# Block rounds of a recurrence and a choice of experts: the inverse of the denominators by an integer guess, a logarithm and an exponential, with the quotient ahead of the choice

## The chip, the cores and the metric

The kernel runs on one core of one Trainium2 chip. The metric is the device time of one execution in microseconds (us). Three runs of the kernel before took 3029.61, 3036.44 and 3038.48 us, median 3036.44.

## The reference

Six layers act in turn on x, 64 x 64 tokens (4096) of 256 channels: a gated linear attention, a recurrence over each sequence, a mixture of 8 experts, a windowed attention, an attention over heads, and a gated perceptron. What the change touches is the second, a weighted mean over the past with per-channel decay w and bonus u:

```python
def step(carry, kv_t):
    p, q, o = carry
    kt, vt = kv_t
    no = jnp.maximum(o, u + kt)
    A = jnp.exp(o - no)
    E = jnp.exp(u + kt - no)
    y = (A * p + E * vt) / (A * q + E)
    no2 = jnp.maximum(w + o, kt)
    A2 = jnp.exp(w + o - no2)
    E2 = jnp.exp(kt - no2)
    return ((A2 * p + E2 * vt, A2 * q + E2, no2), y)
...
x = x + _L0_xattn_ref(64, 64, 256, L0_xattn_w, L0_xattn_u, _layernorm(x, axis=-1), ctx_2048)
x = x + _L0_ffn_ref(_layernorm(x, axis=-1), ...)   # router: logits, top 2 of 8 experts, softmax of the two
```

The choice of experts for a token needs the finished y of that token: it goes into x, x is normalised, and the router is a product with the result.

## The kernel before

The program has four parts one after another. The first layer takes about half of the span. Then come the block rounds (function `recurrence_and_experts`), in which the recurrence and the router are computed together, then the experts' tiles, then layer one. The edit lies in the block rounds, and in one point it reaches into the experts' stage.

**Blocks and rounds.** The 4096 tokens are 8 blocks of 512 tokens (8 sequences of 64). In SBUF a block of the recurrence is a tile of 128 partitions by 1024 elements: 2 groups of 128 channels, 8 sequences, 64 steps. There are ten rounds, written out by the list `STEPS`. In the round i, three blocks are at work: f = i (the front: normalise, transpose, exponentials of the keys), y = i - 1 (the scans, the inverse, the quotient) and r = i - 2 (add y to x, normalise again, router, choice of two experts, destination rows). So y = r + 1 in every full round. The text names a round by its r. Each engine's program is written out in a fixed order; the engines meet at semaphores.

**Names.** `eh` and `fk` are the exponentials of the keys (ScalarE, `k_out`, L1266 and L1271), `ev` and `fv` the same times the values (GpSimd, L1018 and L1025). `qp` and `pp` are the running sums (VectorE, `scans`, L1399 and L1407). `den` = fk + qp (L1403), `num` = fv + pp (GpSimd, L1011). `reciprocal` (L1412) turns den into 1/den on VectorE and `quotient` (L1417) multiplies num with it. `nm` and `rs` are mean and scale of a normalisation (GpSimd, `power`, L1002 and L1004), from VectorE's `statistics`; set 0 of them serves `xn`, the front, set 1 `xh`, the router (both L1258 on ScalarE). `hb` is the transposed xh in SBUF (L1277). `kvs` are keys and values for a later layer, made on TensorE by `cross_kv` (L1160, L1163) and copied out by ScalarE (L1288).

**The loop from round to round.** VectorE: statistics of xn, `weights_low` (splitting of expert weights, L1472), `settle`, `residual` (add y to x), statistics of xh, scans, reciprocal, `choose` (L1421 to L1441: add the router's bias, find the two largest, make the one-hot table `both`), quotient, `place` (L1458 to L1468: ranks within each expert, destination rows `sent_to`). `choose` waits for TensorE's router (L1138), which waits for hb. `place` waits for `ranks` (TensorE, L1149), which waits for `both`. GpSimd: two scatters of the rows of block r - 1 (L1031, each waits for `sent_to`), `power` for xn, fv, two scatters, `power` for xh, num, ev, four scatters, and for r < 4 the subtraction `wd_low` (L1038). Since GpSimd takes its work in order, `power` of the next round stands behind the scatters that wait for `sent_to`.

**ScalarE** in a full round: kvs, xn, kvs, the values vt, xh, eh, fk, hb, two kvs, `te` (the exponential for the weights of the two experts, L1281), and the high parts of weights (L1295, L1300). All its exponentials of this part use one table of functions, loaded once (L1303), in which the tanh of the experts' stage (L1344) is found too.

## Time and profile before

| | |
|---|---|
| median of three runs | 3036.44 us |
| the profiled execution | 3033.89 us |
| its span | 3032.2 us |
| busy in the span: TensorE | 2750.8 us (91%) |
| VectorE | 2487.2 us (82%) |
| GpSimd | 2111.9 us (70%) |
| ScalarE | 1954.2 us (64%) |
| stage of the block rounds | 1480.8 to 1739.5 us, 258.7 us |

The span is from the first to the last instruction on the engines; the execution has 1.7 us around it. In the rows, PE is TensorE, PEld its weight loads, DVE is VectorE, ACT ScalarE, POOL GpSimd and SP SyncE. L1412 is line 1412 of the kernel before; buffer numbers are left out of names. A row of the timeline gives start, duration, engine, line, operation, output and inputs, and in brackets the idle time of the engine before it and what ended that. The busy shares are means over stages that have different limits, so a share of the span says little of the block rounds, which are 9% of it.

### The profile page before, as it was taken

The page shows a single profiled execution, that of the slowest core. Times are in us where ns is not written, and L with a number is a line of the kernel's source. Part 1 is how long each engine was busy: PE and PEld are TensorE (multiplying, and loading weights), DVE is VectorE, ACT ScalarE, POOL GpSimd, SP SyncE. Part 2 cuts the span into 40 slices and gives each one's busy share as a digit, 9 for nine tenths or more (in the row PEclk, how much of TensorE's full clock was granted, in tenths as well). Part 3 has the DMA queues.
Part 4 walks back from the last instruction along what each step waited for, and adds up shares of the span by engine and source line. Part 5 has one row for each costly group of instructions (what it writes and reads, how often), then busy time and mean ns, then how long its engine had stood idle before and what let it go on. Part 6 is the DMA issues. An engine that isn't in the chain of part 4 may idle for free. (4 is left out here: it accounts for less than half of the span.)

```text
span 3032.2 us, 68140 instructions
## 1 busy us (share of the span) xinstructions
PE 2750.8 (91%) x22096; PEld 2295.9 (76%) x22128; DVE 2487.2 (82%) x5452; ACT 1954.2 (64%) x4120; POOL 2111.9 (70%) x2651
## 2 busy tenths in 40 slices
PE   6999999999999999999788499667999999999978
PEld 3888888888888888888555299535777777777767
DVE  6888888888888888888599577468899898989863
ACT  5888878778787877878444155346666666666642
POOL 5897666666666666666468544369888989898870
PEclk9999999999999999999899699768999999999989
DMA  4555444444444444444444399600000000000000
GB/s 144 172 193 169 133 143 139 144 135 146 137 131 153 131 143 132 155 131 128 142 152 146 134 337 333 207 15 18 20 19 27 21 25 24 22 24 22 21 5 11
DMA packets 185881, 340.09 MB, mean 112 GB/s; under 512 B 40668, under 2 KB 104037, under 8 KB 178936
## 3 DMA queue, kind: packets, MB, share of 16 engines
q1 hardware_dynamic: 179448, 319.55, 32.6%
q0 software_dynamic: 6144, 16.79, 1.8%
q8 instruction: 169, 2.77, 0.4%
q14 instruction: 120, 0.98, 0.1%
HBM read 264.68 MB, written 63.19 MB: 108 GB/s over the span
## 5 line engine op out<-in xcount | busy, mean ns | idle before, releaser
L1804 POOL TENSOR_TENSOR l_prod<-l_sco,l_kv 128x256 f32<-128x256 f32 x512 | 369.5, 760 | 36.4 <-DVE l_sco L2311 36.4
L1797 POOL TENSOR_TENSOR l_prod<-l_q,l_kv 128x256 f32<-128x256 f32 x512 | 358.9, 743 | 47.3 <-DVE l_att L2319 47.3
L718 DVE SCALAR_TENSOR_TENSOR a_cq<-a_PQ,a_taps,a_cq 128x504 f32<-128x504 f32 (+2 forms) x384 | 281.7, 734 | 72.7 <-ACT a_cq L584 63.6
L718 DVE SCALAR_TENSOR_TENSOR a_ck<-a_PK,a_taps,a_ck 128x504 f32<-128x504 f32 (+2 forms) x384 | 280.6, 731 | 9.7 <-ACT a_ck L584 0.5
L342 POOL TENSOR_TENSOR a_tq<-a_cq,a_tq 128x512 f32<-128x512 f32 x128 | 165.9, 1296 | 131.2 <-ACT a_tq L590 131.1
L329 POOL TENSOR_TENSOR a_hrs<-a_hve,a_neghalf 128x8 f32<-128x8 f32 x128 | 209.6, 1638 | 25.7 <-DVE a_hve L735 25.2
L485 PE MATMUL a_Y<-a_wo,a_og_parts 128*128 128x256 f32 x1536 | 205.9, 284 | 5.0 <-POOL a_og_parts L336 5.0
L412 PEld LDWEIGHTS a_X<-a_wv,a_xb 128*128 128x128 f32 x1536 | 200.0, 188 | 12.1 <-issue 1.2
L342 POOL TENSOR_TENSOR a_tk<-a_ck,a_tk 128x512 f32<-128x512 f32 x128 | 163.6, 1278 | 62.8 <-ACT a_tk L590 62.8
L412 PE MATMUL a_PQ<-a_x_hi,a_wqk 128*128 (+1 forms) x512 | 194.1, 420 | 12.6 <-issue 11.9
L412 PE MATMUL a_X<-a_wv,a_xb 128*128 128x256 f32 x1536 | 204.2, 282 | 0.8 <-DMA a_xb<-a_x_lo 0.8
L603 ACT ACTIVATE a_hk<-a_PK,a_lncol 128x512 f32<-128x512 f32 x128 | 99.9, 781 | 154.6 <-PE a_PK L504 154.6
L485 PEld LDWEIGHTS a_Y<-a_wo,a_og_parts 128*128 128x128 f32 x1536 | 194.7, 192 | 6.0 <-issue 5.9
L597 ACT ACTIVATE a_nq<-a_TQ,a_hnb,a_hrs 128x128 f32<-128x128 f32 x512 | 192.5, 463 | 1.5 <-POOL a_hnb L332 1.0
L597 ACT ACTIVATE a_nk<-a_TK,a_hnb,a_hrs 128x128 f32<-128x128 f32 x512 | 191.5, 457 | 0.0
L412 PE MATMUL a_X<-a_x_hi,a_wg 128*128 (+1 forms) x512 | 183.5, 399 | 2.3 <-DVE a_og L743 2.3
L412 PE MATMUL a_PK<-a_x_hi,a_wqk 128*128 (+1 forms) x512 | 182.6, 397 | 0.0
L336 POOL TENSOR_TENSOR a_og_parts<-a_og,a_og_parts 128x512 fp32r<-128x512 f32 x128 | 166.7, 1302 | 17.6 <-ACT a_og_parts L610 17.6
L584 ACT ACTIVATE a_cq<-a_PQ,a_taps 128x512 f32<-128x512 f32 x128 | 99.9, 780 | 100.0 <-PE a_PQ L412 100.0
L325 POOL TENSOR_TENSOR a_hm<-a_hst 128x8 f32<-128x8 f32 x128 | 26.7, 209 | 191.9 <-DVE a_hst L724 191.9
L772 DVE TENSOR_TENSOR_SCAN a_em<-a_dr,a_dm 128x256 f32<-128x256 f32 x128 | 160.0, 1250 | 0.0
L2319 DVE TENSOR_REDUCE l_att<-l_prod 128x64 f32<-128x1024 f32 x128 | 151.7, 1206 | 8.2 <-POOL l_prod L1804 8.0
(398 smaller groups left out, 8380.6 us busy)
## 6 DMA issues: line engine op xcount, KB each, us to landing
a_wqk<-qk_parts SPq DMA_DIRECT2D x112, 512.0 KB, 3.4
m_wgu<-gate_up_parts SPq DMA_DIRECT2D x39, 1024.0 KB, 8.1
a_wv<-v_parts SPq DMA_DIRECT2D x56, 512.0 KB, 3.8
a_wg<-g_parts SPq DMA_DIRECT2D x112, 256.0 KB, 3.3
a_wo<-o_parts SPq DMA_DIRECT2D x112, 256.0 KB, 2.9
a_dr<-decays SPq DMA_DIRECT2D x256, 64.0 KB, 2.6
m_hs<-sorted_rows SPq DMA_DIRECT2D x39, 256.0 KB, 7.1
sorted_outs<-m_ys SPq DMA_DIRECT2D x39, 256.0 KB, 7.5
```

Source lines behind the costliest of these rows:

```text
L329: nc.gpsimd.tensor_tensor(out=hrs[q][:], in0=hve[q][:], in1=neghalf[:], op=ALU.pow).then_inc(s_hrstd, 1)
L336: nc.gpsimd.tensor_tensor(out=og_parts[q][:, 1, :], in0=og[q][:], in1=og_parts[q][:, 0, :].bitcast(F32), op=ALU.subtract).then_inc(og_lo, 1)
L342: nc.gpsimd.tensor_tensor(out=t[i][p][:], in0=c[i][p][:], in1=t[i][p][:], op=ALU.mult).then_inc(s_silu, 1)
L412: last = nc.tensor.matmul(out, lhs(i, k), rhs(j, k), start=at_pass == PASSES[0], stop=at_pass == PASSES[-1])
L485: last = nc.tensor.matmul(Y[:, j, :], og_parts[p][:, i, j * P:(j + 1) * P], wo[p][:, w, :], start=first and j % 2 == 0 and k == 0, stop=Tr ...
L584: nc.scalar.activation(c[i][p][:], PB[i][:], ACT.Identity, bias=taps[p][:, bias:bias + 1], scale=taps[p][:, tap + KW - 1:tap + KW]).then_i ...
L597: nc.scalar.activation(nrm[i][q][:, j, :], TB[i][:, j, :], ACT.Identity, bias=hnb[q][:, k:k + 1], scale=hrs[q][:, k:k + 1]).then_inc(s_nor ...
L718: nc.vector.scalar_tensor_tensor(out=acc, in0=src, scalar=taps[p][:, tap + k:tap + k + 1], in1=acc, op0=ALU.mult, op1=ALU.add).then_inc(s_ ...
L772: nc.vector.tensor_tensor_scan(out=flat(em[q]), data0=flat(dr[q]), data1=flat(dm[q]), initial=0.0, op0=ALU.mult, op1=ALU.add).then_inc(s_e ...
L1797: nc.gpsimd.tensor_tensor(out=prod[:, h], in0=qv[:, h:h + 1, :].to_broadcast([P, H, HD]), in1=kk, op=ALU.mult).then_inc(S("E_pqk"), 1)
L1804: nc.gpsimd.tensor_tensor(out=prod[:, h], in0=sco[:, h:h + 1, :].to_broadcast([P, HD, H]), in1=vv, op=ALU.mult).then_inc(S("E_pav"), 1)
L2319: nc.vector.reduce_sum(att[:].rearrange("p (h d) -> p h d", d=HD)[:, 4 * k:4 * k + 4, :], prod[:, 4 * k:4 * k + 4], axis=AX).then_inc(S("E ...
```

## The change

The vector engine's inverse of den is replaced. In `scans`, directly behind den, VectorE makes a first guess `near` of 1/den: it reads den's bits as an integer i and writes 0x7EF311C0 - i as the bits of near. Then it multiplies den by near, which gives a number `left` (kept in den) close to one. ScalarE takes the logarithm of left and the exponential of minus that, which is 1/left, both in place, in a new function `reciprocal` that stands behind `h_out` in its order. VectorE's `quotient` now first waits for this (semaphore `rest`) and multiplies 1/left by near, which gives 1/den, then multiplies num with it as before. `quotient` moves from behind `choose` to ahead of it. A table set that holds both logarithm and exponential is named ahead of the rounds.

```diff
@@ in recurrence_and_experts
+    I32, INVERSE_BITS = mybir.dt.int32, float(0x7EF311C0)
...
-            den, num = own("den", [P, NS, SEQ]), own("num", [P, NS, SEQ])
+            den, num, near = own("den", [P, NS, SEQ]), own("num", [P, NS, SEQ]), own("near", [P, NS, SEQ])
@@ block.scalar
+                def reciprocal(b):
+                    act.wait_ge(S("left"), b + 1)
+                    nc.scalar.activation(den[:], den[:], ACT.Ln).then_inc(S("log"), 1)
+                    act.wait_ge(S("log"), b + 1)
+                    nc.scalar.activation(den[:], den[:], ACT.Exp, scale=-1.0).then_inc(S("rest"), 1)
+
...
+                nc.scalar.preload_act_table_set("natural_log_exp_and_others")
                 act.wait_ge(S("tab"), 5)
...
                     if r is not None:
                         h_out(r)
+                    if y is not None:
+                        reciprocal(y)
                     if f is not None:
                         kv_out(f, (0, 1))
@@ block.vector
                     nc.vector.tensor_tensor(out=den[:], in0=fk[:], in1=qp[:, :, 0:SEQ], op=ALU.add).then_inc(S("den"), 1)
+                    dve.wait_ge(S("den"), b + 1)
+                    nc.vector.tensor_scalar(near[:].bitcast(I32), den[:].bitcast(I32), -1.0, INVERSE_BITS, ALU.mult, ALU.add).then_inc(S("near"), 1)
+                    dve.wait_ge(S("near"), b + 1)
+                    nc.vector.tensor_tensor(out=den[:], in0=den[:], in1=near[:], op=ALU.mult).then_inc(S("left"), 1)
                     dve.wait_ge(S("ev"), b + 1)
...
-                def reciprocal(b):
-                    dve.wait_ge(S("den"), b + 1)
-                    nc.vector.reciprocal(den[:], den[:]).then_inc(S("rec"), 1)
-
                 def quotient(b):
+                    dve.wait_ge(S("rest"), b + 1)
+                    nc.vector.tensor_tensor(out=den[:], in0=den[:], in1=near[:], op=ALU.mult).then_inc(S("rec"), 1)
                     dve.wait_ge(S("rec"), b + 1)
                     dve.wait_ge(S("num"), b + 1)
                     nc.vector.tensor_tensor(out=num[:], in0=num[:], in1=den[:], op=ALU.mult).then_inc(S("y"), 1)
...
                     if y is not None:
                         scans(y)
-                        reciprocal(y)
+                        quotient(y)
                     if r is not None:
                         choose(r)
-                    if y is not None:
-                        quotient(y)
-                    if r is not None:
                         place(r)
```

In what order the instructions stand on an engine is shown for two engines. On VectorE, in the round of r = 0, before (m_qp and m_pp are the running sums, m_lg the router's sums with bias, m_both the one-hot table, m_rank the ranks):

```order
L1399 SCALAR_TENSOR_TENSOR m_qp<-m_keep,m_eh 128x1040
L1403 TENSOR_TENSOR m_den<-m_fk,m_qp 128x1024
L1407 SCALAR_TENSOR_TENSOR m_pp<-m_keep,m_ev 128x1040
L1412 RECIPROCAL m_den<-m_den 128x1024
L1421 TENSOR_TENSOR m_lg<-m_TY,m_rb 128x32
...
L1441 TENSOR_TENSOR m_both<-m_oh 128x32
L1417 TENSOR_TENSOR m_num<-m_num,m_den 128x1024
L1458 TENSOR_TENSOR m_rank<-m_TY,m_start_at 128x32
```

and of the changed kernel, the same place on VectorE:

```order
L1409 SCALAR_TENSOR_TENSOR m_qp<-m_keep,m_eh 128x1040
L1413 TENSOR_TENSOR m_den<-m_fk,m_qp 128x1024
L1415 TENSOR_SCALAR m_near<-m_den 128x1024
L1417 TENSOR_TENSOR m_den<-m_den,m_near 128x1024
L1421 SCALAR_TENSOR_TENSOR m_pp<-m_keep,m_ev 128x1040
L1426 TENSOR_TENSOR m_den<-m_den,m_near 128x1024
L1429 TENSOR_TENSOR m_num<-m_num,m_den 128x1024
L1433 TENSOR_TENSOR m_lg<-m_TY,m_rb 128x32
...
L1453 TENSOR_TENSOR m_both<-m_oh 128x32
L1470 TENSOR_TENSOR m_rank<-m_TY,m_start_at 128x32
```

The guess and a product stand ahead of the second scan, and both products of the quotient stand ahead of the choice; nothing stands between the one-hot table and the ranks any more. On ScalarE, the same round before (m_xh is the normalised block, m_hb its transpose, m_kvs keys and values):

```order
L1258 ACTIVATE m_xh<-x_sb,m_nm,m_rs 128x256 x4
L1266 ACTIVATE m_eh<-m_TK 128x16x64
L1271 ACTIVATE m_fk<-m_TF 128x1024
L1277 ACTIVATE m_hb<-m_TY 128x1024
L1288 ACTIVATE m_kvs<-m_TV 128x512 x2
```

and of the changed kernel on ScalarE:

```order
L1259 ACTIVATE m_xh<-x_sb,m_nm,m_rs 128x256 x4
L1267 ACTIVATE m_eh<-m_TK 128x16x64
L1272 ACTIVATE m_fk<-m_TF 128x1024
L1278 ACTIVATE m_hb<-m_TY 128x1024
L1286 ACTIVATE m_den<-m_den 128x1024
L1288 ACTIVATE m_den<-m_den 128x1024
L1295 ACTIVATE m_kvs<-m_TV 128x512 x2
```

The logarithm and the exponential stand between hb and the copies of keys and values. In the two rounds without a block r yet, of which one has a block y, they stand directly behind fk. The order on TensorE, GpSimd and SyncE is the same as before. One load of a table is added: in the experts' stage, ahead of the first tanh.

## Rows read from the trace of the kernel before

**Rows 1.** Block rounds: length; busy of PE, PEld, DVE, ACT, POOL; clock, DMA, GB/s
```profile
1480.80:1739.50 258.70, 187.76 (x916) 117.79 (x916) 200.15 (x457) 97.10 (x151) 171.56 (x147) 0.84 0.45 157
```

**Rows 2.** By line: duration ns min/median/max, first and last start
```profile
L1412 DVE RECIPROCAL m_den<-m_den x8: 6523/6524/6527, 1512.0 to 1690.5; 128x1024 f32<-128x1024 f32 x8
...
L1417 DVE TENSOR_TENSOR m_num<-m_num,m_den x8: 1215/1218/1225, 1518.5 to 1701.2; 128x1024 f32<-128x1024 f32 x8
...
L1526 DVE TENSOR_SCALAR m_keep<-m_keep,m_wc x2: 479/480/480, 1485.7 to 1486.1; 128x512 f32<-128x512 f32 x2
...
L1303 ACT ACT_TABLE_LOAD  x1: 1283/1283/1283, 1480.8 to 1480.8; - x1
...
L1004 POOL TENSOR_TENSOR m_nm<-m_ng,m_rs x16: 202/204/1249, 1490.9 to 1710.0; 128x4 f32<-128x4 f32 x16
```

**Rows 3.** VectorE's timeline, choice of experts: start us, us, ... [idle before <-releaser]
```profile
1541.95 0.12 DVE L1421 TENSOR_TENSOR m_lg<-m_TY,m_rb 128x32 f32<-128x32 f32 x1
...
1648.29 0.19 DVE L1421 TENSOR_TENSOR m_lg<-m_TY,m_rb 128x32 f32<-128x32 f32 x1 [0.85 <-PE m_TY L1138]
...
1675.12 0.19 DVE L1421 TENSOR_TENSOR m_lg<-m_TY,m_rb 128x32 f32<-128x32 f32 x1 [3.78 <-PE m_TY L1138]
...
1699.34 0.19 DVE L1421 TENSOR_TENSOR m_lg<-m_TY,m_rb 128x32 f32<-128x32 f32 x1 [2.34 <-PE m_TY L1138]
```

**Rows 4.** ScalarE's timeline, round of r = 4
```profile
1641.10 2.08 ACT L1258 ACTIVATE m_xh<-x_sb,m_nm,m_rs 128x256 f32<-128x256 f32 x4 [3.58 <-POOL m_nm L1004]
...
1644.89 1.01 ACT L1277 ACTIVATE m_hb<-m_TY 128x1024 f32<-128x1024 f32 x1
```

**Rows 5.** TensorE's timeline, router of r = 4 and r = 6
```profile
1646.40 1.85 PE L1138 MATMUL m_TY<-m_rw,m_hb 128*128 128x8 f32 x16
...
1695.72 3.58 PE L1138 MATMUL m_TY<-m_rw,m_hb 128*128 128x8 f32 x16 [1.11 <-ACT m_hb L1277]
```

**Rows 6.** VectorE's timeline, round of r = 4; last row from r = 7
```profile
1638.67 2.31 DVE L1407 TENSOR_TENSOR_SCAN m_pp<-m_keep,m_ev 128x1040 f32<-128x1040 f32 x1
...
1650.06 0.19 DVE L1441 TENSOR_TENSOR m_both<-m_oh 128x32 bf16<-128x32 f32 x1
...
1651.31 0.18 DVE L1458 TENSOR_TENSOR m_rank<-m_TY,m_base 128x32 f32<-128x32 f32 x1
...
1652.04 0.17 DVE L1468 CAST m_sent_to<-m_row_of 128x8 uint32<-128x8 f32 x1
...
1720.46 0.19 DVE L1458 TENSOR_TENSOR m_rank<-m_TY,m_base 128x32 f32<-128x32 f32 x1 [0.63 <-PE m_TY L1149]
```

**Rows 7.** GpSimd's and VectorE's timelines: r = 4, then r = 1 and 2
```profile
1639.73 1.25 POOL L1004 TENSOR_TENSOR m_nm<-m_ng,m_rs 128x4 f32<-128x4 f32 x1
...
1641.12 2.18 POOL L1011 TENSOR_TENSOR m_num<-m_fv,m_pp 128x1024 f32<-128x1024 f32 x1
...
1650.40 1.82 POOL L1031 DMA_INDIRECT sorted_rows<-m_xh,m_sent_to  x1 [0.30 <-issue]
...
1568.85 2.35 POOL L1038 TENSOR_TENSOR m_wd_low<-m_wd_low,m_wd_high 128x1024 fp32r<-128x1024 f32 x1
...
1568.57 2.66 DVE L1431 TENSOR_TENSOR m_te<-m_mx 128x4 f32<-128x4 f32 x1
...
1597.50 2.60 DVE L1468 CAST m_sent_to<-m_row_of 128x8 uint32<-128x8 f32 x1
```

**Rows 8.** ScalarE's timeline, before r = 0, and first tanh of the experts
```profile
1517.69 1.02 ACT L1271 ACTIVATE m_fk<-m_TF 128x1024 f32<-128x1024 f32 x1 [2.48 <-PE m_TF L1112]
...
1525.02 2.07 ACT L1258 ACTIVATE m_xn<-x_sb,m_nm,m_rs 128x256 f32<-128x256 f32 x4
...
1747.88 0.63 ACT L1344 ACTIVATE m_th<-m_gp 128x512 f32<-128x512 f32 x1 [3.07 <-DVE m_gp L1571]
```

**Rows 9.** TensorE's timeline, first transposes of the context, two rounds
```profile
1635.39 1.06 PE L1099 MATMUL m_TV<-ident,m_ctx_t 128*128 128x128 f32 x8 [1.66 <-ACT m_kvs L1288]
...
1659.31 1.94 PE L1099 MATMUL m_TV<-ident,m_ctx_t 128*128 128x128 f32 x8 [3.16 <-ACT m_kvs L1288]
```

## The prediction

> **What bounds the kernel now.** I read the stage table first: the block rounds, the only stage the edit touches, take 258.7 us of the 3032.2 us span [rows 1]. VectorE is busy for 200 us of them and no other engine for more, so the page alone would call VectorE the bound, and its eight inverses at 6.52 us each [rows 2], 52 us in all, the thing to take out. Then I read VectorE's timeline of the rounds, looking only at the wait in front of the choice of experts (the sum with the router's bias, which needs TensorE's router matmul). The reader should see there that after the inverse VectorE still stands idle: 0.85, 3.78 and 2.34 us in the rows shown [rows 3]. Of the seven rounds that contain an inverse and a choice (blocks r = 0 to 6), six show such an idle time, and only r = 0 has none. So the inverse ends before the router does: it lies inside a wait. What sets the round is the chain that leads to the router.
>
> That chain, in the round of r = 4, is read on four engines. GpSimd gives the mean and scale (nm, 1639.73 plus 1.25), ScalarE normalises (xh, from 1641.10), TensorE transposes, ScalarE copies the result (hb, 1644.89 to 1645.90) [rows 4, 7], TensorE runs the router (1646.40 plus 1.85) [rows 5], and VectorE chooses at 1648.29 [rows 3]. From the end of hb to the choice it is 2.39 us. The choice itself runs to the end of `both`, 1650.25; then comes the quotient, behind which the ranks on TensorE are hidden, then `rank` at 1651.31, and the destination rows are out at 1652.21 [rows 6]. From hb's end to there: 6.31 us. GpSimd's scatters of the next round, and with them the next normalisation, wait for that last instruction, so the loop closes through it.
>
> **The change, part by part.**
> Removed: 8 inverses, 8 x 6.52 = 52.2 us of VectorE. Added on VectorE per block: one integer guess, `near`, and two products more (`left`, and the one ahead of the old quotient). A product of this shape takes 1.22 us [rows 2]. The guess has no row. Nearest is a tensor_scalar of half the size, 0.48 us [rows 2]; the bounds are 0.48 and, as if it were a product, 1.22; I take 0.9, near twice the half-sized one. VectorE's busy time falls by 6.52 - 2 x 1.22 - 0.9 = 3.2 us per block, 25 us in all (23 to 29 by the bounds). That would be the gain if VectorE were the bound.
>
> Added on ScalarE: a logarithm and an exponential of 128x1024 per block. I price each like hb and fk of the same size, 1.01 and 1.02 us [rows 4, 8], and take 1.05 with the wait between the two; the exponential can hardly differ from fk, which is one. The logarithm has no row; I allow it half of fk's time to twice that time. Their place matters more than their length: they stand behind fk and hb in ScalarE's order, although the denominators are ready several us earlier. In the round of r = 4 they start when hb ends, 1645.90, and end at 1648.0.
>
> Moved: the quotient now stands ahead of the choice and waits for that exponential. Queued behind it on VectorE are the choice, the ranks and the destination rows, that is, the loop. Two products of 1.22 us bring VectorE to 1650.4, where it starts the choice it started at 1648.29 before: 2.1 us late, with the router's result waiting since 1648.25. The choice takes its 1.96 us, to 1652.4. Then the ranks on TensorE, which the old quotient covered, are bare: in the one round with nothing behind `both` (r = 7), that wait is 0.63 us [rows 6]. From `rank` to the end it is 0.90 us. So the destination rows are out at 1653.9 to 1654.0 instead of 1652.21: **+1.7 us per round that is bound by the router.** This is the main term.
>
> Where that applies. r = 4 and 5: 2 x 1.7 = 3.4 us. r = 6: the router ran 3.58 us instead of 1.85 [rows 5], so its choice came 1.7 us later after hb than that of r = 4, and most of the new chain is covered; +0.4. r = 0: before, its choice followed the inverse without idle time [rows 3], but in the round before it ScalarE now has the pair behind fk, which ended at 1518.72 [rows 8]. VectorE's two products then end at 1523.3 instead of the one at 1519.7, the next statistics follow them, and the normalisation that began at 1525.02 [rows 8] begins near 1526.4; with the chain after hb this comes to +1.9. r = 7 has no inverse: 0.
>
> r = 1, 2, 3: here GpSimd subtracts weights (wd_low, 2.35 us) at the end of its round, and a small VectorE instruction is held for all of it: 2.66 us for a 128x4 difference, 2.60 us for a 128x8 cast [rows 7]. Such an operation takes 0.17 us at other times [rows 6], so the collision costs 2.4 us per round before. After the change, VectorE's second scan comes later by the guess and a product, 2.1 us; the numerator on GpSimd (2.18 us, from 1641.12 in r = 4 [rows 7]) waits for it and starts at 1643.1. Then the weighting, again 2.18, four scatters of 0.96 and 0.30 between them, one of them held behind the products as in the row with 1.82 [rows 7]: 1653.5, and wd_low ends at 1655.9. In the same coordinates it was 1652.2 + 2.4 = 1654.6. Whether it catches VectorE's last instructions or only makes GpSimd late for the next round, the next scatters start there: +1.3, three times, 3.9 us. Bounds: -0.7 each if GpSimd slips in earlier and nothing collides, +3 each if both the collision and the lateness are paid.
>
> The clock. In the round of r = 5, TensorE's first transposes of the context start after 3.16 us of idle time and take 1.94 us against 1.06 in the round before, where it had stood idle for 1.66 [rows 9]: the lower of its two levels, 1.2 GHz, for some us, and the choice of that round shows 3.78 us of idle time for it [rows 3]. I put that at 2.4 us for this round (3.78 us of idle time where there were 0.85, less the 0.5 that VectorE came earlier) and allow half as much for each of the two other rounds with idle times over 2 us, 4.5 us together. After the change the ranks come later, and with them the block that fills TensorE in front of this gap, which shrinks to about 2.4 us. I give back half: -2.2, bounds -4.5 and +3.
>
> The table of functions. The set with both logarithm and exponential is loaded once, where a set was loaded before. Tanh now needs a load of 1.28 us [rows 2] in the experts' stage, and ScalarE is idle for 3.07 us there, waiting for VectorE [rows 8]: 0. The Trainium skill (ScalarE: Activation LUTs, "What ACT_TABLE_LOAD costs") puts a switch at about 2.66 us with its drain, of which the row shows the load alone; that too would fit into the wait.
>
> **Sum**: 3.4 + 0.4 + 1.9 + 3.9 - 2.2 = +7.4 us, against the profiled execution's own 3033.9 us: 3041.3. That execution lies 2.5 us under the median of the runs, 3036.44, and inside their spread. I forecast 3041 us. 0.3%, 9.1 us, is about what a measurement can tell from no change here, so this is inside it, on the slow side.
>
> **Rivals.**
> 1. VectorE was the bound after all, or the exponential is not late: then the whole 25 us of its time comes off, 3009 us; or half, if the later rounds fall back on the router, 3020. For it: VectorE's 200 us of 258.7, and rounds in which its idle time is only 0.85. Against it: the idle rows, and the order, in which VectorE must wait for ScalarE behind hb. 0.12.
> 2. Contention, the other side. In r = 4, nm takes 1.25 us although it takes 0.20 at the least: it ends with VectorE's scan, 1640.98 [rows 2, 6, 7]. The inverse, one input, let GpSimd's numerator run beside it at its full 2.18 [rows 7]. Now guess, `left` and the scan follow each other without a break. If nm has to wait for the last of them, xh starts 2.1 us later, and hb, the router and everything else with it. In the five rounds r = 1 to 5 that is +10 on top of 7.4: 3051 us, slower. It decides as soon as GpSimd loses more than 0.3 us per round before xh, since then the total passes 9.1. For it: the stretched nm. Against it: two instructions more mean two gaps more in which GpSimd can slip in, and nm already waits until 1640.98, which is when `left` ends in the new order. 0.20.
> The Trainium skill says in SBUF — State Buffer, "SBUF: two separate sides", that one pair of ports is an exclusive lock between VectorE and GpSimd, taken also by VectorE operations with two SBUF inputs, and that the loser blocks fully. By that rule this rival is what exchanging an inverse for products does. The stretched nm and the held cast agree with it, but they don't tell who wins a gap.
> 3. Nothing adds up: collisions miss, the clock gives 4.5 back, 3034 us. For it: each bound above is wide. 0.13.
> 4. It doesn't do what it says: a table load for each logarithm and each exponential, 16 x 1.28 = 20 us, 3062. The order of instructions shows one load for the rounds. 0.01.
>
> **How the numbers follow.** My forecast has 0.54 with its own range 3034 to 3048, of which a third lies past 9.1 us from 3033.9. Faster: rival 1, 0.12, and 0.01 of the rest. Slower: rivals 2 and 4, 0.21, and about 0.12 of the forecast, 0.33. Same: 0.54. The range for 8 in 10 takes in rivals 2 and 3 and, for the executions' own spread of some 4 us, a little more: 3026 to 3053; it leaves out rival 1 and the far end of rival 2.
>
> **What would show it.** The inverse's rows are gone; VectorE's busy time is down by 25 us with the span unchanged or longer; a new wait of VectorE on ScalarE's exponential of about 4 us per round, and none left on the router; a wait of about 0.6 us on the ranks; the choice starts 4.5 us after hb ends; wd_low ends later against hb by 3 us. I am wrong if VectorE doesn't wait at the quotient, if the distance from hb's end to the destination rows is not near 8 us, if nm moves against the statistics, or if the stage gets shorter than 250 us.

## The result and the profile after

The changed kernel took 3046.68 us (median of 20 runs, 3038.54 to 3054.96), the kernel before 3037.62 us on the same chip (20 runs). The ratio is 1.003 with a 95% interval of 1.0019 to 1.0042, or 9.1 us: slower by a little, with the sign and the mechanism of the forecast and near its size (own sum +7.4 us, forecast 3041, range 3026 to 3053). The median lies 5.7 us over the forecast; 1.7 us of that are the sum's, and most of the rest is its base, a profiled execution of 3033.89 us that was 3.7 us quicker than the median before. The prediction drew its line between no change and slower at 9.1 us and gave 0.54 to the one and 0.33 to the other. The difference fell on that line, so it says nothing for or against those two chances.

The profiled execution took 3046.16 us (before 3033.89), its span is 3044.4 us (3032.2), 12.2 us more. The block rounds after, in the view that gives busy time by stretch (columns as in [rows 1]):

```profile
1482.80:1751.50 268.70, 190.93 (x916) 117.25 (x916) 175.03 (x473) 113.20 (x167) 172.17 (x147) 0.83 0.43 151
```

VectorE lost 25.1 us of busy time and the stage became 10.0 us longer [rows 1]. The stage starts 2.0 us later, ahead of anything that the edit touches. From here on, "the stage" is measured from VectorE's first product of `weights_low` to the end of the last destination rows (`sent_to`) of r = 7, in one profiled execution of each kernel: 216.25 us before, 226.16 after, +9.9. The rest of this text compares that number.

VectorE's timeline of the round of r = 4, and behind the first "..." that of r = 7, answer to [rows 3] and [rows 6]:

```profile
1649.65 0.69 DVE L1415 TENSOR_SCALAR m_near<-m_den 128x1024 int32<-128x1024 int32 x1
1650.38 1.22 DVE L1417 TENSOR_TENSOR m_den<-m_den,m_near 128x1024 f32<-128x1024 f32 x1
1651.52 2.32 DVE L1421 TENSOR_TENSOR_SCAN m_pp<-m_keep,m_ev 128x1040 f32<-128x1040 f32 x1
1658.01 1.35 DVE L1426 TENSOR_TENSOR m_den<-m_den,m_near 128x1024 f32<-128x1024 f32 x1 [4.18 <-ACT m_den L1288]
1659.40 1.23 DVE L1429 TENSOR_TENSOR m_num<-m_num,m_den 128x1024 f32<-128x1024 f32 x1
1660.54 0.18 DVE L1433 TENSOR_TENSOR m_lg<-m_TY,m_rb 128x32 f32<-128x32 f32 x1
...
1662.37 0.19 DVE L1453 TENSOR_TENSOR m_both<-m_oh 128x32 bf16<-128x32 f32 x1
1663.16 0.19 DVE L1470 TENSOR_TENSOR m_rank<-m_TY,m_base 128x32 f32<-128x32 f32 x1 [0.60 <-issue]
...
1663.90 0.17 DVE L1480 CAST m_sent_to<-m_row_of 128x8 uint32<-128x8 f32 x1
...
1729.76 0.19 DVE L1433 TENSOR_TENSOR m_lg<-m_TY,m_rb 128x32 f32<-128x32 f32 x1 [9.07 <-PE m_TY L1139]
```

ScalarE's timeline of the same round (to compare with [rows 4]):

```profile
1654.93 1.02 ACT L1278 ACTIVATE m_hb<-m_TY 128x1024 f32<-128x1024 f32 x1
1655.83 1.06 ACT L1286 ACTIVATE m_den<-m_den 128x1024 f32<-128x1024 f32 x1
1656.92 1.06 ACT L1288 ACTIVATE m_den<-m_den 128x1024 f32<-128x1024 f32 x1
```

`left` is ready at 1651.60, but ScalarE takes the logarithm only when hb is done. The exponential ends at 1657.98, and VectorE, idle for 4.18 us until then, starts the first product at 1658.01. The choice, which has no idle time before it any more, starts 4.6 us after hb's end (1655.95), and the destination rows are out at 1664.07, 8.1 us after it. In the round of r = 7, which has no inverse, the choice still waits for the router, as before.

The first product of r = 0 on VectorE's timeline, and on GpSimd's the subtraction of weights beside it and `nm` of r = 1:

```profile
1544.12 3.02 DVE L1426 TENSOR_TENSOR m_den<-m_den,m_near 128x1024 f32<-128x1024 f32 x1 [4.80 <-ACT m_den L1288]
...
1563.30 1.23 DVE L1417 TENSOR_TENSOR m_den<-m_den,m_near 128x1024 f32<-128x1024 f32 x1
```

```profile
1543.71 2.35 POOL L1039 TENSOR_TENSOR m_wd_low<-m_wd_low,m_wd_high 128x1024 fp32r<-128x1024 f32 x1
...
1563.52 1.07 POOL L1005 TENSOR_TENSOR m_nm<-m_ng,m_rs 128x4 f32<-128x4 f32 x1
```

And the waits of VectorE between 1510 and 1740 us (engine, what waited, for what: us in total, times, longest), the largest first:

```profile
DVE m_den L1426 <- ACT m_den L1288: 41.0, 8, 6.4
DVE m_lg L1433 <- PE m_TY L1139: 9.1, 1, 9.1
...
DVE m_rank L1470 <- PE m_TY L1150: 4.3, 7, 0.6
```

The time taken out of VectorE has become a wait of VectorE: 41 us for the exponential. Before, it waited 12.8 us for the router in the rounds of r = 1 to 6; that wait is gone.

### The profile page after: what moved, and what is told of

It reads as the page before. It is cut to its first block and busy times, and to the rows that moved or that the text cites. A ratio compares the mean times of both kernels' runs of the same rounds, so it can differ in the third digit from the quotient of the medians.

```text
span 3044.4 us, 68205 instructions
## 1 busy us (share of the span) xinstructions
PE 2758.3 (91%) x22128; PEld 2298.7 (76%) x22128; DVE 2465.9 (81%) x5468; ACT 1971.2 (65%) x4137; POOL 2111.4 (69%) x2651
## 5 line engine op out<-in xcount | busy, mean ns | idle before, releaser
L412 PE MATMUL a_PQ<-a_x_hi,a_wqk 128*128 (+1 forms) x512 | 195.6, 423 | 12.0 <-issue 11.3
```

Source lines behind the costliest of these rows:

```text
L412: last = nc.tensor.matmul(out, lhs(i, k), rhs(j, k), start=at_pass == PASSES[0], stop=at_pass == PASSES[-1])
```

## The experiments

Every kernel was timed side by side with the kernel before: the changed one in 20 executions, e3 and e7 in 6, e4 in 8, the others in 12. The stage is one reading each. "Loop part" below is the time from the end of hb to the end of the destination rows of a round; "time to the next hb" runs from there to the end of the next round's hb.

| kernel | median us (before) | ratio, 95% interval | stage us |
|---|---|---|---|
| before | | | 216.25 |
| changed | 3046.68 (3037.62) | 1.003, 1.0019 to 1.0042 | 226.16 |
| e1 | 3052.08 (3036.24) | 1.0044, 1.0029 to 1.0058 | 229.14 |
| e2 | 3036.32 (3036.24) | 1.0004, 0.9991 to 1.0017 | 215.93 |
| e3 | 3048.33 (3036.24) | 1.0039, 1.0025 to 1.0053 | 225.01 |
| e4 | 3049.23 (3036.24) | 1.0034, 1.0022 to 1.0046 | 224.59 |
| e5 | 3043.90 (3037.84) | 1.0016, 1.0001 to 1.0031 | 221.16 |
| e6 | 3032.66 (3037.84) | 0.9987, 0.997 to 1.0003 | 211.66 |
| e7 | 3059.63 (3037.84) | 1.0058, 1.0043 to 1.0072 | 235.66 |
| e9 | 3041.46 (3037.84) | 1.0006, 0.9994 to 1.0018 | 219.58 |
| e11 | 3028.41 (3036.73) | 0.9975, 0.9964 to 0.9985 | 207.63 |
| e12 | 3036.25 (3036.73) | 1.0007, 0.9995 to 1.0018 | 215.56 |
| e13 | 3043.35 (3036.73) | 1.0025, 1.001 to 1.0039 | 221.69 |
| e14 | 3032.65 (3036.73) | 0.9992, 0.998 to 1.0005 | 212.27 |

### Is it the order, or what stands in it?

**e1**, the changed kernel with the quotient back behind the choice:

```diff
                         scans(y)
-                        quotient(y)
                     if r is not None:
                         choose(r)
+                    if y is not None:
+                        quotient(y)
+                    if r is not None:
                         place(r)
```

> The changed kernel with its quotient put back behind the choice of experts; the inverse still goes through ScalarE. The stage is read in the trace from the first splitting of weights by VectorE to the last destination rows: 216.3 us before, 226.2 us changed. Theory (the loop runs through hb, router, choice, destination rows, and whatever stands between them costs its length): the choice starts 2.4 us after hb's end again, but two products (2.4 us) now stand where one stood, in place of the bare wait for the ranks. Destination rows 7.6 us after hb's end, against 8.0 changed and 6.3 before: 0.4 us per round less than the changed kernel, stage 223 us, total 3 us under the changed one. Rival (the order is the fault, not the second product): the distance returns to 6.3, stage 216. Rival (VectorE's relief shows once the wait is gone): stage under 210, total 10 us or more under before.

A miss: the wait was gone, but the stage was 229.14 us, 6 over the 223 expected and 3 over the changed kernel's. Round of r = 4 on VectorE's timeline (hb ended at 1658.12):

```profile
1660.97 0.19 DVE L1433 TENSOR_TENSOR m_lg<-m_TY,m_rb 128x32 f32<-128x32 f32 x1 [8.16 <-PE m_TY L1139]
...
1662.75 0.19 DVE L1453 TENSOR_TENSOR m_both<-m_oh 128x32 bf16<-128x32 f32 x1
1662.86 1.22 DVE L1426 TENSOR_TENSOR m_den<-m_den,m_near 128x1024 f32<-128x1024 f32 x1
1664.11 1.23 DVE L1429 TENSOR_TENSOR m_num<-m_num,m_den 128x1024 f32<-128x1024 f32 x1
1665.25 0.18 DVE L1470 TENSOR_TENSOR m_rank<-m_TY,m_base 128x32 f32<-128x32 f32 x1
...
1665.98 0.17 DVE L1480 CAST m_sent_to<-m_row_of 128x8 uint32<-128x8 f32 x1
```

The choice comes 2.85 us after hb, but two products instead of one lie between `both` and `rank`, and the wait for TensorE's ranks that they hide is only 0.6 us. The loop part is 8.0 us again; in the rounds of r = 1 to 3 it is 10.9, 10.9 and 9.9. There the subtraction of weights holds the first of the two products (4.05 us in the round of r = 1) or a small instruction behind them. So "put the quotient where it was" is no remedy.

**e2**, the kernel before with only the order changed:

```diff
                         reciprocal(y)
-                    if r is not None:
-                        choose(r)
-                    if y is not None:
                         quotient(y)
                     if r is not None:
+                        choose(r)
                         place(r)
```

> The kernel before, with only its quotient moved ahead of the choice; inverse on VectorE. Theory: in a round like r = 4 the inverse ends at 1647.4 and the quotient would end at 1648.65, against the choice at 1648.29: 0.4 us late, then the ranks are bare (0.63 us) in place of the quotient's 1.14. Stage 215 to 218 us, no difference from before within 2 us. So the order alone costs nothing with an inverse that is ready in time. Rival (the order is what costs the changed kernel its time): stage 226, as changed.

215.93 us against 216.25, ratio 1.0004: the new order by itself costs nothing. In the rounds of r = 1 to 5 the old quotient fits into the idle time ahead of the choice, which starts 2.7 to 2.9 us after hb; in those of r = 0 and 6 it does not, and the loop part is 1.0 and 1.7 us longer. Over all rounds, the loop parts are 1.4 us longer and the times to the next hb 1.7 shorter. In the changed kernel the order costs, because the new quotient cannot start before ScalarE is through.

### What is the pair on ScalarE worth?

**e3**, the changed kernel without logarithm and exponential. The product stays uncorrected, so y is wrong, and other experts can be chosen: only its stage is compared.

```diff
@@ block.scalar
-                    if y is not None:
-                        reciprocal(y)
@@ block.vector, quotient
-                    dve.wait_ge(S("rest"), b + 1)
+                    dve.wait_ge(S("left"), b + 1)
```

> The changed kernel without ScalarE's logarithm and exponential: the quotient uses the guess corrected by nothing, so y is only near the reference's; everything else, both products and the order, stays. Theory: the wait of VectorE at the quotient goes and the choice starts when the router is done, 2.4 us after hb's end; destination rows after 5.9 instead of 8.0: 2.1 us off in each of six rounds and some in r = 0, stage 211 to 214 us, total 12 to 15 us under changed and 3 to 5 under before. That is what an inverse at no cost would be worth. Rival (VectorE is the bound and its own instructions decide): stage as changed, 226, since VectorE's work is the same. Rival (contention with GpSimd decides): stage above 222.

A miss: stage 225.01 us, 11 to 14 more than expected and in the range of the rival that contention with GpSimd decides, although the loop part was between 6.4 and 7.2 us in six of the eight rounds. What was won there was lost between the destination rows and the next hb: in two rounds this took 23.5 and 23.2 us. GpSimd's timeline in the second of them, where r = 3's destination rows were out at 1640.32:

```profile
1640.84 2.38 POOL L1039 TENSOR_TENSOR m_wd_low<-m_wd_low,m_wd_high 128x1024 fp32r<-128x1024 f32 x1
1643.38 1.93 POOL L1032 DMA_INDIRECT sorted_rows<-m_xh,m_sent_to  x1 [0.17 <-issue]
...
1650.39 3.02 POOL L1032 DMA_INDIRECT sorted_rows<-m_xh,m_sent_to  x1 [0.17 <-issue]
...
1654.70 1.99 POOL L1003 TENSOR_TENSOR m_rs<-m_ve,m_neghalf 128x4 f32<-128x4 f32 x1
1656.77 1.25 POOL L1005 TENSOR_TENSOR m_nm<-m_ng,m_rs 128x4 f32<-128x4 f32 x1
```

GpSimd has no idle time here beyond its gaps of issue. There is a second loop, GpSimd's own order, that stands ready when the first is shortened. From the destination rows to the end of `nm` it took 17.7 us here, 12.7 in the kernel before. The subtraction now starts behind the destination rows, and VectorE stretches what follows: a scatter of 0.96 us takes 3.02, and `rs`, 1.37 us in the same place before, takes 1.99. (`nm` took 1.25 us before, too [rows 7].)

**e4**, the changed kernel with the pair ahead of hb on ScalarE:

```diff
-                    if r is not None:
-                        h_out(r)
                     if y is not None:
                         reciprocal(y)
+                    if r is not None:
+                        h_out(r)
```

> The changed kernel with ScalarE's logarithm and exponential ahead of hb instead of behind it. Theory: where ScalarE has no gap ahead of hb, hb and with it the router come 2.0 us later, the quotient no longer makes the choice wait, and the choice starts 2.4 us after the later hb: 4.4 us after where hb ended, as now (4.5). In rounds in which ScalarE waits for TensorE in front of hb, a part of the pair is hidden. Stage 222 to 227 us, total as changed or up to 4 us less. Rival (only the quotient's wait costs, a later router does not): stage 214.

As expected: the choice comes 2.04 us after hb in four of the eight rounds, but hb comes later (in the first five rounds 19.4 to 20.8 us after the destination rows, where it was 17.6 to 18.7), and the stage is 224.59 us. The pair costs about the same on either side of hb.

### How much is the subtraction of weights?

**e5** and **e6** move the four subtractions `wd_low` from the rounds of r = 0 to 3 to those of r = 6 and 7, two each; e5 in the changed kernel, e6 in the kernel before:

```diff
-                    if r is not None and r < 4:
-                        down_low(r)
+                    if r is not None and r >= 6:
+                        down_low(2 * (r - 6))
+                        down_low(2 * (r - 6) + 1)
```

> The changed kernel with the four weight subtractions of GpSimd (wd_low) moved from the rounds r = 0 to 3 to the ends of rounds r = 6 and 7, two each, where GpSimd is idle for 4.7 and 6.1 us. Theory (two loops side by side: the chain over hb, and GpSimd's own queue of about as many us, which wd_low lengthens and in which it holds small VectorE instructions): the holds of 1.8 to 2.8 us in r = 0 to 3 go, destination rows 8.0 us after hb's end in all rounds; stage 216 to 219 us against 226, total 7 to 10 us under changed. Rival (the second loop is not wd_low but contention in general): stage 223 or more.

> The kernel before with the same move of wd_low. Theory: the holds of 2.4 us in r = 1, 2 and 3 go and nothing else is bound in them; destination rows 6.3 to 6.8 us after hb's end; stage 208 to 211 us against 216, total 5 to 8 us under before. Rival (GpSimd merely waits at the next thing, and VectorE, full in these rounds, becomes the bound): stage 213 to 216.

e5 came to 221.16 us, 2.2 above the range expected, e6 to 211.66, 0.7 above it. In e5 the loop part is 7.9 to 8.1 us in the rounds of r = 0 to 5. In that of r = 6 it is 12.97, since VectorE's last instruction there ran into two subtractions in a row (VectorE's timeline, then GpSimd's, same kernel):

```profile
1702.72 4.87 DVE L1481 CAST m_sent_to<-m_row_of 128x8 uint32<-128x8 f32 x1
```

```profile
1702.91 4.63 POOL L1039 TENSOR_TENSOR m_wd_low<-m_wd_low,m_wd_high 128x1024 fp32r<-128x1024 f32 x2
```

A cast of 0.17 us took 4.87. This place was a bad choice of mine, and e11 and e12 mend it. By the totals, e6 cannot be told from the kernel before: its interval holds 1.

**e9** takes out both, the pair as in e3 and the subtractions as in e5:

> The changed kernel without ScalarE's logarithm and exponential (y only near the reference's, as in the run without the pair) and with wd_low moved to r = 6 and 7. The run without the pair alone had stage 225.0 us although destination rows came 6.5 to 7.2 us after hb's end; in two of its rounds nm was 5 us late. Theory (its gain on the one loop was lost on GpSimd's queue, and wd_low is what makes that queue the longer one): with wd_low gone from r = 1 to 3 the gain of 2.1 us per round appears, stage 200 to 206. Rival (products and scan of VectorE hold GpSimd's scatters and nm whatever wd_low does): the late nm stays and the stage is above 212.

A clear miss: 219.58 us, where the rival that VectorE holds GpSimd in any case had "above 212". With the subtractions away, GpSimd should have had the time; it did not. GpSimd's timeline in the round of r = 2, and VectorE's beside it:

```profile
1585.43 3.02 POOL L1032 DMA_INDIRECT sorted_rows<-m_xh,m_sent_to  x1 [0.17 <-issue]
...
1589.74 1.99 POOL L1003 TENSOR_TENSOR m_rs<-m_ve,m_neghalf 128x4 f32<-128x4 f32 x1
1591.81 1.25 POOL L1005 TENSOR_TENSOR m_nm<-m_ng,m_rs 128x4 f32<-128x4 f32 x1
1593.20 3.02 POOL L1012 TENSOR_TENSOR m_num<-m_fv,m_pp 128x1024 f32<-128x1024 f32 x1
```

```profile
1585.28 2.31 DVE L1408 TENSOR_TENSOR_SCAN m_qp<-m_keep,m_eh 128x1040 f32<-128x1040 f32 x1
...
1589.61 1.23 DVE L1416 TENSOR_TENSOR m_den<-m_den,m_near 128x1024 f32<-128x1024 f32 x1
1590.75 2.32 DVE L1420 TENSOR_TENSOR_SCAN m_pp<-m_keep,m_ev 128x1040 f32<-128x1040 f32 x1
1592.99 1.20 DVE L1425 TENSOR_TENSOR m_den<-m_den,m_near 128x1024 f32<-128x1024 f32 x1
```

The scatter, issued 0.15 us after the first scan's start, ends at 1588.45, when that scan (1587.59) is over by 0.86 us; `nm` ends at 1593.06, with the second scan (1593.07); the numerator ends at 1596.22, 2.03 us after the product at 1592.99 is done (1594.19). The scatter and the numerator are held until VectorE's operation with two inputs from SBUF is over and then take about their own time; `nm` ends when the scan does. So the normalisation xh starts at 1593.18 and the time to the next hb is 20.3 to 20.8 us in three rounds.

The kernel to compare with is e6, which has the old inverse, and the subtractions where e9 has them (both lose time to them in the round of r = 6): its stage is 211.66 us, 7.9 shorter. The loop parts of the two add up to the same within 0.3 us, but from the destination rows to the end of `nm` e9 takes 9.4 us more in all. In the round shown it is 15.4 us against 12.7. Of these 2.7 us, 1.0 have come up by the end of the `nm` for xn, since GpSimd reaches the new scatters late, and 1.7 come up behind it, with the holds. An inverse that costs nothing on ScalarE, and half the time on VectorE, thus gains nothing: with the pair (e5) the stage is 9.5 us longer than in e6, without it (e9) 7.9. What the late quotient loses on the one loop, the operations put in place of the inverse lose on the other: the second scan and so the numerator come later, and more of GpSimd's work is held. These two were not separated.

The Trainium skill says in SBUF — State Buffer, "SBUF: two separate sides", that of a GpSimd operation and a VectorE operation with two SBUF inputs, or in a 2-port mode, the one that starts first holds the shared ports for the whole instruction and the other fully blocks. The scatter and the numerator here agree: VectorE's operation with two inputs started 0.15 and 0.21 us ahead of them. The cast of e5 was held too, but its recorded start (1702.72) is ahead of the subtractions' (1702.91), and it was held through both of them; so the rows do not show that the first to start wins, and none shows in what mode a cast with one input runs.

**e7** lets the quotient of a block wait until the next round, behind the statistics of xn, and puts the numerator on GpSimd behind the four scatters; subtractions as in e5:

```diff
@@ block.gpsimd
+                    if r:
+                        scatter(r - 1, slice(4, 2 * BT))
...
-                    if r:
-                        scatter(r - 1, slice(4, 2 * BT))
@@ block.vector
+                    if r is not None:
+                        quotient(r)
...
                         scans(y)
-                        quotient(y)
```

> The changed kernel's inverse over ScalarE, with nothing of it between hb and the destination rows: VectorE's quotient stands in the next round behind the statistics of xn, GpSimd's last four scatters stand ahead of its numerator and weighting, and wd_low is in r = 6 and 7. Theory: destination rows 5.9 us after hb's end (2.4 to the choice, 1.96, 0.6, 0.9); VectorE has its first products 2 us after them, the sum into x comes 2.5 us later than in the kernel before, which GpSimd's power for xh, 10 us behind the destination rows, still covers. Rounds of 23.5 to 25 us, stage 200 to 206, total 10 to 15 us under before. Rival (the later sum into x and the later scans pass the cover): the distance of 5.9 appears but the next hb comes 2 us later or more; stage 212 to 218.

The largest miss: 235.66 us, 24.0 more than e6, which has the subtractions in the same place and the inverse on VectorE. The loop part, expected at 5.9 us, is 6.3 to 8.8 in the rounds of r = 0 to 5, and the time to the next hb adds 16.5 us to that of e6. Most of this, 14.6 us, lies between the destination rows and the end of `nm`, which take 15.0 us in five rounds and 12.7 in e6. VectorE's timeline shows why:

```profile
1615.16 1.22 DVE L1430 TENSOR_TENSOR m_num<-m_num,m_den 128x1024 f32<-128x1024 f32 x1
...
1617.44 2.32 DVE L1459 TENSOR_SCALAR m_te<-m_te 128x4 f32<-128x4 f32 x1
...
1620.09 1.28 DVE L1402 TENSOR_TENSOR x_sb<-m_TY,x_sb 128x512 f32<-128x512 f32 x2
```

The sum into x starts 8.1 us after the destination rows (1612.01), 3.5 in e6: two products stand ahead of it, and a `te` of 0.16 us is held for 2.32 beside GpSimd's fv. The statistics and `nm` follow the sum. What comes on top, 1.9 us in all, stands on TensorE's timeline:

```profile
1616.44 1.97 PE L1125 MATMUL m_TY<-ident,m_num 128*128 128x128 f32 x8 [3.15 <-DVE m_num L1430]
...
1618.87 3.78 PE L1165 MATMUL m_TV<-m_wkv,m_vt 128*128 128x512 f32 x4
...
1623.43 1.07 PE L1101 MATMUL m_TV<-ident,m_ctx_t 128*128 128x128 f32 x8 [0.78 <-ACT m_kvs L1296]
```

The transpose of y waits 3.15 us for the late quotient and then takes 1.97 us, where the transposes of the same shape in the last row take 1.07: the granted clock is 0.50 there and 1.00 in the last row, the lower of the two clocks, 1.2 GHz, and the higher. The keys and values stand behind it, and behind them the transposes that the next front needs. I had moved the quotient out of one part of the loop and into another.

### The price alone, and a better kernel

**e11** and **e12** move the four subtractions behind the rounds, into GpSimd's wait at the start of the experts' stage; e11 in the kernel before, e12 in the changed one:

```diff
-                    if r is not None and r < 4:
-                        down_low(r)
...
+                for n in range(4):
+                    down_low(n)
```

> The kernel before with GpSimd's four weight subtractions (wd_low) behind the rounds, after its first three copies of biases, where it is idle for 16 us before the experts' first tile. With them at the ends of r = 6 and 7 the stage was 211.7 us, of which r = 6 and 7 had lost 4 us to holds of VectorE. Theory: stage 206 to 209 us against 216.3, total 6 to 10 us under before; the four subtractions, 9.4 us, end before the experts need them. Rival (the experts' stage pays for it): the stage falls, and the experts start or proceed later by as much; total as before.

> The changed kernel with the same move. Theory: destination rows 8.0 us after hb's end in every round, as in the run with wd_low in r = 6 and 7, without that run's 5 us loss there: stage 214 to 217 us. Against the kernel before with the same move 7 to 9 us slower: the price of the change itself, with no collision on either side, 6 x 1.2 to 1.7 us. Rival (the change's price was mostly collisions with wd_low): the two agree within 3 us.

e11 is the fastest kernel of all, 0.9975 (0.9964 to 0.9985) of the kernel before, 8.3 us less by the medians; it beats both. e12 takes 7.8 us more than e11 by the medians, and its stage is 7.9 us longer. Without the subtractions in the rounds, this is the price of the change with no collision with them. The round of r = 1 in e11 (hb ended at 1563.06), VectorE:

```profile
1565.91 0.19 DVE L1421 TENSOR_TENSOR m_lg<-m_TY,m_rb 128x32 f32<-128x32 f32 x1 [2.41 <-PE m_TY L1138]
...
1569.66 0.17 DVE L1468 CAST m_sent_to<-m_row_of 128x8 uint32<-128x8 f32 x1
```

and in e12 (hb ended at 1570.25):

```profile
1572.31 1.23 DVE L1426 TENSOR_TENSOR m_den<-m_den,m_near 128x1024 f32<-128x1024 f32 x1 [6.20 <-ACT m_den L1288]
...
1574.72 0.18 DVE L1433 TENSOR_TENSOR m_lg<-m_TY,m_rb 128x32 f32<-128x32 f32 x1
...
1578.02 0.17 DVE L1480 CAST m_sent_to<-m_row_of 128x8 uint32<-128x8 f32 x1
```

6.77 us against 7.94. Over the eight rounds the loop part is 7.3 us longer in e12, the first round starts 1.8 us later, and 1.1 us come back between the destination rows and the next hb: 8.0 us, of 7.9 measured.

**e13** regroups the product: num times near first, which needs nothing from ScalarE, then times 1/left:

```diff
-                    dve.wait_ge(S("rest"), b + 1)
-                    nc.vector.tensor_tensor(out=den[:], in0=den[:], in1=near[:], op=ALU.mult).then_inc(S("rec"), 1)
...
-                    nc.vector.tensor_tensor(out=num[:], in0=num[:], in1=den[:], op=ALU.mult).then_inc(S("y"), 1)
+                    nc.vector.tensor_tensor(out=near[:], in0=num[:], in1=near[:], op=ALU.mult).then_inc(S("rec"), 1)
+                    dve.wait_ge(S("rec"), b + 1)
+                    dve.wait_ge(S("rest"), b + 1)
+                    nc.vector.tensor_tensor(out=num[:], in0=near[:], in1=den[:], op=ALU.mult).then_inc(S("y"), 1)
```

> The changed kernel with its quotient regrouped: numerator times guess first, while VectorE waits for ScalarE, then that times ScalarE's 1/left. The same values up to rounding, the same instructions, but only one product of 1.22 us behind the exponential. Theory (what stands between hb and the destination rows costs its length): 1.2 us less per round in seven rounds, destination rows 6.8 us after hb's end where nothing collides, stage 217 to 221 us against 226. Rival (the second product only fills a wait for something else, or GpSimd's queue is the bound now): stage 224 or more. Some of it can be lost, since the first product can now be held while GpSimd weights.

**e14** does the same, with num times near ahead of the choice, the last product behind it, and the subtractions as in e12:

```diff
                         scans(y)
-                        quotient(y)
+                        guessed(y)      # num times near, into near
                     if r is not None:
                         choose(r)
+                    if y is not None:
+                        quotient(y)     # waits for rest; near times 1/left, into num
+                    if r is not None:
                         place(r)
```

> All together: inverse over ScalarE, numerator times guess ahead of the choice, the last product behind the choice (where it covers the wait for the ranks), wd_low behind the rounds. Theory: the distance from hb's end to the destination rows is as in the kernel before, 6.3 to 6.8 us, and VectorE has 2 us less per round, which is worth nothing: stage 206 to 210 us, equal within 3 us to the kernel before with wd_low behind the rounds, total 5 to 10 us under before. Rival (ScalarE's pair delays something else, such as the copies of keys and values): 212 or more. Rival (VectorE's relief is worth something once it is not waiting): 203 or less.

e13 came close to what was expected (221.69 us, 0.7 over the range and 4.5 less than the changed kernel). e14 has the loop part of the kernel before, 6.3 to 6.8 us in the first six rounds, and still takes 212.27 us, 2.3 above the range I expected, just inside that of the rival "212 or more", and 4.6 above e11. The time to the next hb is 19.9 us in the round of r = 1 and 20.3 in that of r = 4. The latter on TensorE's timeline, GpSimd's and ScalarE's:

```profile
1631.62 1.75 PE L1100 MATMUL m_TV<-ident,m_ctx_t 128*128 128x128 f32 x8 [4.16 <-ACT m_kvs L1295]
```

```profile
1631.29 3.02 POOL L1032 DMA_INDIRECT sorted_rows<-m_xh,m_sent_to  x1 [0.17 <-issue]
```

```profile
1639.04 2.08 ACT L1259 ACTIVATE m_xh<-x_sb,m_nm,m_rs 128x256 f32<-128x256 f32 x4 [4.61 <-POOL m_nm L1005]
```

A held scatter and transposes at the lower clock stand side by side there, but hb waits for the scatter's side. `nm` ends 15.4 us after the destination rows, against 12.7 in e11, and from there to hb it is 4.9 us, against 6.1. Over all rounds, the way from the destination rows to the end of `nm` is 4.1 us longer than in e11 (2.7 in r = 4, 2.1 in r = 6), that from there to the next hb 0.3 longer (1.4 in r = 1, most of it given back in other rounds), the first hb comes 1.0 later, and the loop parts give back 0.8: 4.6 us. So it is again GpSimd's order that takes most of the gain. The rival named for this run, that the pair delays something else, can stand behind the first hb and the 1.4 us of r = 1; no run separates it.

## Why the prediction was right, and where its terms were off

**The bound.** The inverse was inside a wait and the chain over hb was the bound: right, and shown by e2 (the order free) and by the stage of the changed kernel, 25 us less work and 10 us more time. Rival 1 (VectorE the bound) is out. One thing was missing: the loop through GpSimd's order stands close behind the loop over hb. e3, e9 and e14 show that it takes over as soon as the latter is shortened. That does not touch the forecast, but it does touch what would have been said of a repair.

**The costs on the engines.** The guess took 0.69 us, within the bounds of 0.48 to 1.22 and below the 0.9 taken. Logarithm 1.05 us and exponential 1.06, as taken. VectorE's busy time: -25.1 in the block rounds, -21.3 over the span, forecast -25. The wait for the exponential was 4.2 us in the round of r = 4 and 5.1 on average, forecast about 4.

**The loop part.** Choice 4.5 us after hb: 4.47 to 4.8 in the rounds of r = 1 to 6. Destination rows 8.0 after it: 7.95 to 8.12 in the rounds of r = 4 to 6, where nothing collides. A wait of 0.6 on the ranks: 0.60. All right. But the term of +1.7 us per round was too large. It was read from one round, in which the router's result came 2.39 us after hb; in others it comes 2.85 us after it. In e12 against e11 the five rounds r = 1 to 5 give 1.2, 1.6, 1.4, 1.2 and 1.1, 1.3 on average. In the changed kernel itself, r = 4 and 5 gave 1.8 and 1.2, 3.0 against 3.4. r = 6: +0.4, as forecast, although a step to it was misread: before, the choice of that round came 3.67 us after hb against 2.39 in r = 4, so 1.3 us later and not 1.7.

**r = 0.** Forecast +1.9, measured +4.0. The start (first hb) is 1.8 later, by the way that was forecast: VectorE waits 6.4 us for the pair, and xn starts 2.3 us later in the stage (forecast 1.4). This with the rest of the chain is what was worked out: e12 against e11 has +2.2 in this round. What failed is that no collision was counted there: the subtraction of weights at 1543.71 held the first product for 3.02 us instead of 1.23. That is 1.8 us, and the largest error of the sum.

**r = 1 to 3.** Forecast +3.9 for `wd_low`. The loop parts of these rounds grew by 1.6, 2.0 and 0.6 us, 4.2 in all, but for another reason. Each of them has one small instruction held for some 2.4 us before, and one after (`both` 2.98, the cast 2.61, `te` 2.21 us). e12 against e11, without subtractions, has +1.2, +1.6 and +1.4 in the same loop parts, 4.2 again. So behind this term is the plain lengthening of the loop, which the sum had left out in these three rounds; that a lateness of `wd_low` was booked with nearly the same number was luck. `wd_low` ended later against hb by 2.5, 2.0 and 1.2 us, where 3 was forecast. In the whole stage, the subtractions cost 8.6 us before (216.25 - 207.63) and 10.6 after (226.16 - 215.56), so they got dearer by 2.0, most of which is the one collision of r = 0.

**The clock.** Forecast -2.2; from the destination rows to the next hb, the sum over the rounds fell from 120.4 to 118.7 us, -1.6. The idle time of TensorE ahead of the context's transposes fell from 15.5 to 11.3 us in seven rounds, as foreseen. The granted clock in the first 4.7 us of the front's transposes in the round of r = 5, before and after (columns as in [rows 1]):

```profile
1659.30:1664.00 4.70, 4.69 (x16) 3.67 (x17) 4.67 (x3) 1.02 (x1) 4.29 (x4) 0.50 0.84 323
...
1671.20:1675.90 4.70, 4.70 (x29) 3.61 (x30) 4.60 (x6) 1.02 (x1) 4.30 (x4) 1.00 0.84 325
```

From the end of `nm` to that of hb, this round took 7.4 us before and 4.9 after. But the lower clock came up elsewhere. In the round of r = 3 of the changed kernel, TensorE stood idle for 3.44 us ahead of the ranks, since `both` came late, and then had the granted clock 0.50 from 1636.6 to 1642.5, where it was 0.71 before, behind 2.23 us of idle time; the same way in the round of r = 4 took 1.4 us longer than before. Over the whole stage the mean clock was 0.87 before and 0.86 after. So a gain in one round was in part paid for in another, and that the sum came near the forecast is not the forecast's working. That had a slip, too: half of 2.4 us for two more rounds makes 4.8 and not 4.5, and there were three such rounds, not two (idle times of 2.39, 2.54 and 2.34 us).

**The sum.** As measured: 4.0 (r = 0) + 4.2 (r = 1 to 3) + 3.0 (r = 4 and 5) + 0.4 (r = 6) - 1.6 = +10.0 us, of 9.9 in the stage, against +7.4 forecast.

**The chances.** A third of 0.54 is 0.18; the prediction then counts 0.12 of it as slower, so its 0.33 for slower should have been 0.39.

**The table.** Cost 0, right. ScalarE's timeline at the first tanh:

```profile
1756.93 1.28 ACT L1354 ACT_TABLE_LOAD   x1
1759.98 0.63 ACT L1354 ACTIVATE m_th<-m_gp 128x512 f32<-128x512 f32 x1 [1.77 <-DVE m_gp L1580]
```

The 3.07 us of waiting for VectorE [rows 8] have become a load of 1.28 and a wait of 1.77.

**Rival 2**, a late `nm`, did not come as it was priced. In the round of r = 1, `nm` ends at 1564.59, with `left` (1564.53), not with the second scan. Its mechanism is real all the same: e9 shows it, with `nm` held to the end of the second scan. **Rivals 3 and 4**, that nothing adds up or that each logarithm and each exponential loads a table, did not come: the stage grew by 9.9 us, and the trace of the changed kernel has one load for the rounds and the one ahead of the first tanh.

## What to carry to other kernels

Before shortening a long operation, look whether the next instruction on its engine waits for something else anyway; if so, shortening it gains nothing, and what it is traded for may cost. An operation given to another engine stands behind what that engine, working in order, does for the loop, and so can join the loop. Then look for the loop that stands closest behind the first: here it ran through GpSimd, and it took what e3, e9 and e14 had won. Work that nobody waits for belongs where its engine is idle and no instruction of the loop runs beside it: moving four subtractions gave 8.3 us, rewriting eight inverses of 6.52 us lost 9.1.

## What the runs showed of the hardware

- A tensor_scalar on 128x1024 int32 took 0.69 us on VectorE, where a product of two inputs of that size took 1.22.
- A small VectorE operation beside GpSimd's subtractions can take as long as these: 4.87 us for a cast of 0.17. The other way round, VectorE's scan or product stretched an indirect scatter from 0.96 to 3.02 us and the numerator of 2.18 us to 3.02. The inverse, with one input, did not hold GpSimd's numerator beside it, which took 2.18 us [rows 7]; replacing one such operation by several, most of them with two inputs, thus had a price on the other engine (e9 against e6: 9.4 us more between the destination rows and `nm`).
- TensorE's transposes of the context took 1.06 us at a granted clock of 1.00 and 1.94 at 0.50 [rows 9].
